# Order of the first two token groups in the K/V stage of a pre-norm transformer layer

## The reference

```
k = layernorm(x) @ wk + bk      # [4096, 2048] x [2048, 512]
v = layernorm(x) @ wv + bv      # the same shape
```

## Time and profile before

| | us |
|---|---|
| median of 3 runs | 2394.8 (2394.18 to 2396.35) |
| the profiled execution's own time | 2397.82 |
| its span (slowest core, core 6) | 2396.3 |
| the other cores' spans | 2388.2 to 2394.7 |
| K of group 2 begins on core 6 | 119.11 after the span's start |
| group 2 of stage A, with `own_ln` beside it | 32.17 (119.11 to 151.28) |
| group 3, without it | 32.17 (151.28 to 183.45) |
| one step of `own_ln` on VectorE | 1.22 |

### The profile page before, as it was taken

How to read it: one execution, slowest core, us unless ns; L and a number is a source line. 1 busy time by engine, 2 the same in 40 slices (tenths; PEclk the granted TensorE clock), 3 DMA queues, 4 the chain that set the end, 5 groups by cost and what they waited for, 6 DMA issues and landing times.

```text
span 2396.3 us, 32016 instructions; the slowest of 8 cores (2388.2 to 2396.3 us)
## 1 busy us (share of the span) xinstructions
PE 2319.0 (97%) x11140; PEld 1016.3 (42%) x11364; DVE 824.9 (34%) x1505; ACT 621.6 (26%) x789; POOL 78.6 (3%) x148
## 2 busy tenths in 40 slices
PE   5899999999999999999999999999999999999999
PEld 2344433333333443444444444444444444444444
DVE  2432245566554335323333332111333333333101
ACT  1444437777776332111111110000111111110000
POOL 2000000000000000000000000000000000000000
PEclk9999999999999999999999999999999999999999
DMA  9624111111355830522443237776223442234872
GB/s 160 104 36 71 18 27 19 19 19 27 66 84 107 193 112 1 100 52 51 84 84 61 45 57 140 163 165 148 50 53 65 84 79 47 48 74 85 184 158 89
DMA packets 57285, 193.46 MB, mean 81 GB/s; under 512 B 10246, under 2 KB 14854, under 8 KB 48940
## 3 DMA queue, kind: packets, MB, share of 16 engines
q0 software_dynamic: 23808, 139.99, 34.1%
q1 hardware_dynamic: 33324, 51.40, 6.7%
HBM read 306.18 MB, written 25.18 MB: 138 GB/s over the span
## 4 chain that ended last, share of the span: by engine, by line
PE 90%; DMA 3%; issue 2%; ACT 2%; DVE 1%; another core or an unknown queue 1%; POOL 0%; DVEq 0%; ACTq 0%; SPq 0%; POOLq 0%
PE pq L1275 32%; PE pq L1437 15%; PE pq L900 5%; PE pq L729 5%; PE pq L453 4%; PE pq L414 4%; PE pq L628 4%; PE pq L1302 4%; PE pq L1287 4%; PE pq L1353 4%; PE pq L781 4%; DMA wkv_wv<-wv_h 2%; PE pq L799 2%; DMA out_d<-dx_stg 1%; ACT wc_p L742 1%
## 5 line engine op out<-in xcount | busy, mean ns | idle before, releaser
L1275 PE MATMUL pq<-dv_xln,dw_wsl 128*128 128x512 bf16 x3513 | 804.7, 379 | 4.3 <-ACT ds_s L1320 0.3
L1275 PEld LDWEIGHTS pq<-dv_xln,dw_wsl 128*128 128x128 bf16 x3584 | 350.2, 98 | 424.5 <-issue 3.7
L1437 PE MATMUL pq<-dx_x2s,dw_wsl 128*128 128x512 bf16 x1754 | 388.4, 379 | 5.6 <-DVE dx_stg L1455 2.2
L1320 ACT ACTIVATE ds_s<-pq 128x512 bf16<-128x512 f32 x112 | 66.9, 597 | 939.1 <-PE pq L1302 884.3
L1337 DVE TENSOR_TENSOR ds_x<-ds_s,pq 128x512 bf16<-128x512 bf16 x108 | 74.3, 688 | 650.6 <-PE pq L1302 614.8
L742 ACT ACTIVATE wc_p<-pq,gl_nb 128x1024 bf16<-128x1024 f32 (+4 forms) x252 | 256.2, 1046 | 71.9 <-PE pq L729 65.6
L1437 PEld LDWEIGHTS pq<-dx_x2s,dw_wsl 128*128 128x128 bf16 x1792 | 174.7, 98 | 216.8 <-issue 7.2
L1455 DVE TENSOR_TENSOR dx_stg<-pq,dx_stg 128x512 f32<-128x512 f32 x64 | 42.0, 688 | 334.6 <-PE pq L1437 141.9
L781 PE MATMUL pq<-wc_p,pp_V 128*128 128x512 bf16 (+3 forms) x493 | 139.6, 363 | 1.1 <-DVE pl_p L753 0.2
L1287 PE MATMUL pq<-dp_c,dw_wsl 128*128 128x512 bf16 x438 | 131.1, 379 | 2.2 <-DVE dp_d L1098 1.7
L1302 PE MATMUL pq<-dp_d,dw_wsl 128*128 128x512 bf16 x440 | 131.3, 379 | 1.6 <-DVE xg_x L1328 1.0
(11 more groups left out here) (183 smaller groups left out, 1750.6 us busy)
## 6 DMA issues: line engine op xcount, KB each, us to landing
dw_wsl<-w_h POOLq DMA_DIRECT2D x56, 1216.0 KB, 10.0
dw_wsl<-w2b_h POOLq DMA_DIRECT2D x16, 960.0 KB, 10.8
dw_wsl<-w2a_h POOLq DMA_DIRECT2D x16, 896.0 KB, 9.6
wa_xr<-x_tiles POOLq DMA_DIRECT2D x6, 2048.0 KB, 40.2
wc_wq<-wq_h POOLq DMA_DIRECT2D x16, 512.0 KB, 5.7
dw_ev<-xo_oc SPq DMA_DIRECT2D x32, 256.0 KB, 6.1
wo_w<-wo_h POOLq DMA_DIRECT2D x16, 512.0 KB, 14.8
xres_d<-dw_ev SPq DMA_DIRECT2D x32, 256.0 KB, 6.1
```

The lines of the kernel that those rows point to most:

```text
L1275: ms = [(lambda hc, bank=bank, wo_=wo_: (lambda e: e.matmul(bank[:, 0:TD], w[:, wo_ + hc * 128: wo_ + (hc + 1) * 128], xln2[tt][:, hc * TD ...
L1437: ms.append((lambda j=j, t=t: (lambda e: e.matmul(banks[t][:, 0:TD], w[:, j * 128:(j + 1) * 128], x2s[:, j * 2 * TD + t * TD: j * 2 * TD + ...
```

## The change

It moves work of groups 0 and 1 and changes banks; the arithmetic of every product stays the same.

- **Loads:** x of group 1 is asked for ahead of W_v.
- **Group 1's K directly behind group 0's.** Its four heads use `pb[4]`, `pb[5]`, `pb[0]`, `pb[1]`. Heads 0 and 1 are computed in pieces, between the steps of group 0's `moments`, `turn_row`, `k_out` and `k_norm`; heads 2 and 3 whole.
- **W_v's column sums** come behind `moments(1)`, in `pb[2]`; their copy goes to a buffer of its own, `csv`, that lies over V rows of group 6.
- **V of both groups behind that**, in `pb[2]` and `pb[3]`. The four centrings of W_v on VectorE alternate with `k_out(1, p)`. From group 2 on K is in `pb[0]` to `pb[3]` and V in `pb[4]`, `pb[5]`, as before.
- **`own_ln`** of groups 0 and 1 runs during groups 2 and 3 instead of 1 and 2.
- `moments` now calls `put` once, between its copy (L360) and its two matmuls.

```diff
-        c_k, c_v = pb[0:4], pb[4:6]
+        def k_bank(j, kv):
+            return (pb[4], pb[5], pb[0], pb[1])[kv] if j == 1 else pb[kv]
+        def v_bank(j, sub):
+            return pb[(2 if j < 2 else 4) + sub % 2]
...
-        def moments(j, put=(lambda i: None)):
+        def moments(j, put=(lambda: None)):
...
             v = P.g('vector', [lambda e: e.tensor_copy(stA, st_b[:, 0:CK])], waits=[('pe', s1_pe[j])], inc='ve')
+            put()
...
-            put(0)
...
-            put(1)
...
         wk_tok = load_w(wk_sb, wk_h, 'K')
         load_x(0)
+        load_x(1)
         wv_tok = load_w(wv_sb, wv_h, 'V')
-        for j in range(1, 5):
+        for j in range(2, 5):
             load_x(j)
...
-        tot = col_sums(wv_sb, wv_tok, c_v[1])
-        wvs = P.g('scalar', [lambda e: e.activation(out=rs_t[1], in_=c_v[1][:, 0:512], func=AF.Copy)],
-                  waits=[tot], inc='sc')
-        moments(0, lambda i: centre(wv_sb, i, rs_t[1], ('sc', wvs), 'v'))
-        for sub in range(2):
-            v_mm(0, sub, 0, 4)
+        kp1 = {}
+        def k_piece(p):
+            for kv in range(2):
+                kp1[kv] = k_mm(1, kv, 4 * p, 4 * p + 4)
+        squares(1, 0)
+        moments(0, lambda: k_piece(0))
+        squares(1, 1)
+        sums(1, 0)
+        k_piece(1)
         trn = turn_row(0)
-        squares(1, 0)
-        for p in range(1, 4):
...
-        squares(1, 1)
-        v_out(0, 2, v_mm(0, 2))
+        turned(0, trn)
+        k_out(0, 0, kp0[0])
+        k_out(0, 1, kp0[1])
         sums(1, 1)
+        squares(1, 2)
+        k_piece(2)
+        k_out(0, 2, kp0[2])
+        k_out(0, 3, kp0[3])
         k_norm(0)
-        squares(1, 2)
-        v_out(0, 3, v_mm(0, 3))
         sums(1, 2)
         squares(1, 3)
-        for j in range(1, NCK):
+        k_piece(3)
+        kp1[2] = k_mm(1, 2)
+        sums(1, 3)
+        def third_k():
+            kp1[3] = k_mm(1, 3)
+        moments(1, third_k)
+        for p in range(4):
+            tot = col_sums(wv_sb, wv_tok, pb[2], p, [('sc', kb_sc[(0, 2)])] if p == 0 else [])
+        csv_sc = P.g('scalar', [lambda e: e.activation(out=csv, in_=pb[2][:, 0:512], func=AF.Copy)],
+                     waits=[('pe', tot)], inc='sc')
+        trn = turn_row(1)
+        turned(1, trn)
+        for p in range(4):
+            centre(wv_sb, p, csv, ('sc', csv_sc), 'v')
+            k_out(1, p, kp1[p])
+            vpe = [v_mm(0, sub, 4 * p, 4 * p + 4) for sub in range(2)]
+        k_norm(1)
+        v_out(0, 0, vpe[0])
+        v_out(0, 1, vpe[1])
+        for sub in range(2, 4):
+            v_out(0, sub, v_mm(0, sub))
+        squares(2, 0)
+        for sub in range(4):
+            v_out(1, sub, v_mm(1, sub))
+            sums(2, sub)
+            if sub < 3:
+                squares(2, sub + 1)
+        for j in range(2, NCK):
...
-                if j == 1 and kv == 2:
-                    turned(1, turn_row(1))
-                if j <= 2:
-                    own_ln(j - 1, kv)
+                if j <= 3:
+                    own_ln(j - 2, kv)
```

More of the change, by code:

```diff
@@ L179, in build_program @@
         bvr_sb = WA.al('bvr', [128, 512], F32)
+        csv = Arena(nc, SB0 + 58 * KBB, SB0 + 60 * KBB, 'vs').al('csv', [128, 512], F32)
         rbA = [V_sb[:, 28 * 512 + j * 1024:28 * 512 + (j + 1) * 1024] for j in range(2)]
@@ L313, in load_w, with col_sums @@
                                          src[:, p * 2048:(p + 1) * 2048], sem=f'd{tag}{p}')) for p in range(4)]
[L315 to L321, removed]
+        def col_sums(w, toks, bank, p, free=()):
+            return P.g('tensor', [(lambda hc: (lambda e: e.matmul(
+                bank[:, 0:512], onb_sb, w[:, hc * 512:(hc + 1) * 512],
+                start=(hc == 0), stop=(hc == NCH - 1), skip_group_check=True)))(hc)
+                for hc in range(4 * p, 4 * p + 4)], waits=[toks[p], ('dC1', d_c1), *free], inc='pe')
         def centre(w, p, total, tok, key):
@@ L407, in k_mm @@
             wts = []
-            if kv == 0 and j == 0:
+            if j == 0 and kv == 0:
                 wts += [x_tok[0][lo // 4], ('ve', ctr_ve[('k', lo // 4)])]
-            elif kv == 0:
+            elif j == 1:
+                wts.append(x_tok[1][(hi - 1) // 4])
+            elif j >= 2 and kv == 0:
                 wts += x_tok[j]
-            if j and lo == 0:
+            if lo == 0 and j == 1:
+                wts.append(('ve', ctr_ve[('k', 3)]) if kv < 2 else ('sc', kb_sc[(0, kv - 2)]))
+            elif lo == 0 and j == 2:
+                wts.append(('sc', kb_sc[(1, kv + 2)]) if kv < 2 else ('ve', vev_ve[(1, kv)]))
+            elif lo == 0 and j:
                 wts.append(('sc', kb_sc[(j - 1, kv)]))
             return P.g('tensor', [(lambda hc: (lambda e: e.matmul(
-                c_k[kv][:, 0:CK], wk_sb[:, hc * 512 + kv * 128: hc * 512 + (kv + 1) * 128],
+                k_bank(j, kv)[:, 0:CK], wk_sb[:, hc * 512 + kv * 128: hc * 512 + (kv + 1) * 128],
                 x_view(j)[:, hc, :], start=(hc == 0), stop=(hc == NCH - 1), skip_group_check=True)))(hc)
@@ L421, in k_out @@
             kv_ve[(j, kv)] = P.g('vector', [
-                lambda e: e.tensor_mul(c_k[kv][:, 0:CK], c_k[kv][:, 0:CK], rs_t[j % 2]),
+                lambda e: e.tensor_mul(k_bank(j, kv)[:, 0:CK], k_bank(j, kv)[:, 0:CK], rs_t[j % 2]),
             ], waits=[('pe', pe), ('sc', rs_sc[j])], inc='ve')
@@ L425, in k_out @@
             kb_sc[(j, kv)] = P.g('scalar', [
-                lambda e: e.activation(out=ks, in_=c_k[kv][:, 0:CK], func=AF.Identity, bias=bk_sb[:, kv:kv + 1]),
+                lambda e: e.activation(out=ks, in_=k_bank(j, kv)[:, 0:CK], func=AF.Identity, bias=bk_sb[:, kv:kv + 1]),
             ], waits=[('ve', kv_ve[(j, kv)]), ('dCon', d_consts)], inc='sc')
@@ L449, in v_mm @@
             if n == 0:
-                wts.append(('ve', ctr_ve[('v', lo // 4)]))
-            elif n >= 2:
+                wts += [('ve', ctr_ve[('v', lo // 4)]), ('sc', csv_sc)]
+            elif n == 1:
+                wts.append(('sc', kb_sc[(0, 3)]))
+            elif 8 <= n < 10:
+                wts.append(('sc', kb_sc[(1, n - 8)]))
+            else:
                 wts.append(('ve', vev_ve[((n - 2) // 4, (n - 2) % 4)]))
             v_pe[j] = P.g('tensor', [(lambda hc: (lambda e: e.matmul(
-                c_v[sub % 2][:, 0:512], x_view(j)[:, hc, sub * 128:(sub + 1) * 128],
+                v_bank(j, sub)[:, 0:512], x_view(j)[:, hc, sub * 128:(sub + 1) * 128],
                 wv_sb[:, hc * 512:(hc + 1) * 512],
@@ L462, in v_out @@
             vev_ve[(j, sub)] = P.g('vector', [lambda e: e.scalar_tensor_tensor(
-                V_sb[:, ci * 512:(ci + 1) * 512], c_v[sub % 2][:, 0:512], rtok[j % 2][:, sub:sub + 1], bvr_sb,
+                V_sb[:, ci * 512:(ci + 1) * 512], v_bank(j, sub)[:, 0:512], rtok[j % 2][:, sub:sub + 1], bvr_sb,
                 op0=ALU.mult, op1=ALU.add)],
@@ L478, in build_program @@
         load_x(0)
+        load_x(1)
         wv_tok = load_w(wv_sb, wv_h, 'V')
-        for j in range(1, 5):
+        for j in range(2, 5):
             load_x(j)
         z_ve = P.g('vector', [lambda e: e.memset(nsw, 0.0)], inc='ve')
-        tot = col_sums(wk_sb, wk_tok, c_v[0])
         for p in range(4):
-            centre(wk_sb, p, c_v[0][:, 0:512], tot, 'k')
+            tot = col_sums(wk_sb, wk_tok, pb[4], p)
+        for p in range(4):
+            centre(wk_sb, p, pb[4][:, 0:512], ('pe', tot), 'k')
@@ L486, in build_program @@
         for p in range(4):
             squares(0, p)
-            kpe = [k_mm(0, kv, 4 * p, 4 * p + 4) for kv in range(NKV)]
+            kp0 = [k_mm(0, kv, 4 * p, 4 * p + 4) for kv in range(NKV)]
             sums(0, p)
-        tot = col_sums(wv_sb, wv_tok, c_v[1])
-        wvs = P.g('scalar', [lambda e: e.activation(out=rs_t[1], in_=c_v[1][:, 0:512], func=AF.Copy)],
-                  waits=[tot], inc='sc')
-        moments(0, lambda i: centre(wv_sb, i, rs_t[1], ('sc', wvs), 'v'))
-        for sub in range(2):
-            v_mm(0, sub, 0, 4)
@@ L498, in build_program @@
-        trn = turn_row(0)
-        squares(1, 0)
-        for p in range(1, 4):
[L501 to L510, removed]
-        squares(1, 1)
-        v_out(0, 2, v_mm(0, 2))
+        kp1 = {}
@@ L524, in build_program @@
                 if kv == 0:
-                    if j == 1:
-                        sums(1, 3)
                     moments(j)
```

## The result

The changed kernel's median is 2424.09 us (16 runs), that of the kernel before beside it 2395.61 (16 runs). Every comparison here leaves out the runs in which a whole die was slower (5 of the changed kernel's 16), and the ratio of the rest is 1.0062, interval 1.0040 to 1.0085. That ratio holds two things: of the 11 runs seven lie at 2400.7 to 2403.1, median 2402.2, and four at 2424 to 2426, in which one or two pairs of neighbouring cores (2 and 3, 6 and 7) were 20 us and more longer at a granted clock of 0.983. Two further series of the same kernel had no such run in 17 and gave 1.0024 (1.0014 to 1.0033) and 1.0022 (1.0011 to 1.0032): **slower by 5 to 6 us, clear of noise and just over 0.2%**.

The account below looks back on a forecast made before the run. TensorE, busy 97% of the span, was taken as the bound. Group 2 at 116.8 at full clock plus 3.6 for clock falls gives 120.4, against the mean core's 117.65 +2.75: 2394.8 + 2.8 = 2397.6 us, range 2392.5 to 2402.

Parts of the forecast that it names:

- Loads* (1): Load queue: x of group 1 takes W_v's early places, W_v lands by about 64 us, and no load is waited for.
- Dense part* (4): TensorE from k_norm(0) to W_v's column sums: 15.3 us without a wait, ending at 77.1; 4.5 us of W_v waits gained.
- Gaps* (2, 3, 5, 6): TensorE idles 2.95 us before sums(1, 0), 6.0 before k_norm(0), 3.0 around turn_row(1), 3.2 between V pieces, 1.8 around k_norm(1).
- the stretch at full clock, with its waits: From the end of K of group 0, 43.8, to the start of group 2, 116.8, without any clock fall.
- fall at the first gap: Lower clock behind the 2.95 us wait ahead of sums(1, 0): half of 1.6, 0.8 us.
- fall at the second gap: Lower clock behind the 6.0 us wait ahead of k_norm(0), with dense work following: 2.6 us.
- fall at the third gap: Lower clock behind the wait around turn_row(1), mostly hidden by VectorE's pace of 2.8: 0.2 us, at most 0.9.
- The term for the clock: Slower matmuls behind the three gaps, in sum 3.6 us, moving the start of group 2 from 116.8 to 120.4.
- the first rival: Every gap fells the clock at full price, 6.1 us: group 2 at 122.9, kernel 2400.1; chance 0.29.
- no fall: Rival: no clock fall on the path, group 2 at 116.8, kernel 2393.9; chance 0.18.
- no queueing at k_norm: Rival: ScalarE gets the k_out pairs in ahead, so the 6.0 us gap and its 2.6 go: 2389.0; chance 0.05.
- x lands late: Rival: x of group 1 arrives late and TensorE waits behind K of group 0, up to 8 us: 2403; chance 0.03.

Follow-up runs that it names:

- a0: The changed kernel again beside the kernel before: stretch (end of K of group 0 to start of group 2) 78.6 us, ratio 1.0024.
- a7: The changed kernel once more, unaltered, beside the kernel before, to look for the cluster at 2424: stretch 78.5 us, ratio 1.0022.
- a5: The changed kernel with only the loads in their old order, W_v ahead of x of group 1: ratio 1.0074, group 2 starts at 135.2.
- b1: The changed kernel with all three gaps filled together by reordering K pieces, k_norm, column sums, centrings and V pieces: 2386.04 us, ratio 0.9958, stretch 64.1.
- b4: The changed kernel with only k_norm(1) moved behind V's third and fourth block: stretch 76.8 us, ratio 1.0011.
- a4: The changed kernel with 24 matmuls that nothing reads added in the gap ahead of k_norm(0): stretch 76.6 us, ratio 1.0016.
- a1: The changed kernel with k_norm(0) moved behind the fourth K piece and head two of group 1: stretch 76.1 us, ratio 1.0007.
- b2: b1 with k_norm(0) and the sums put back ahead of the K piece and head two: stretch 71.4 us, ratio 0.9993.
- a3: The changed kernel with the second K piece of group 1 put ahead of sums(1, 0): stretch 76.6 us, ratio 1.0013.
- a2: The changed kernel with W_v's column sums and three of four centrings moved ahead of head two of group 1: stretch 79.0 us, ratio 1.0020.

## Why the prediction was wrong

**The steps that held, in kind.** *Loads* (1): no wait for W_v, and x of group 1 in time. *Dense part* (4): no wait. *Gaps* (2, 3, 5, 6): all of them stand where the walk had them, on the engines that it named, and the V pieces are 2.8 apart. own_ln and everything from group 2 on: no change, as forecast (core 0 of the changed kernel takes 32.16 and 32.17 us for groups 2 and 3).

**What failed is two sizes in the sum.** The table sets what the sum took beside what the stretch holds, as the mean of the eight cores, in the first profile and in those of a0 and a7.

| us | taken | first | a0, a7 |
|---|---|---|---|
| the stretch at full clock, with its waits | 73.0 | 74.7 | 74.7, 74.7 |
| fall at the first gap | 0.8 | 2.1 | 1.6, 1.4 |
| fall at the second gap | 2.6 | 1.7 | 1.4, 1.6 |
| fall at the third gap | 0.2 | 0 | 0, 0 |
| fall on V's 48 matmuls behind k_norm(1) | none | 1.1 | 0.8, 0.8 |
| sum | 76.6 | 79.6 | 78.6, 78.5 |

- **The term for the clock, 3.6 us at three places, was 4.9, 3.9 and 3.8.** Two of its parts were too small. For the first gap I took half of 1.6 because core 0 of the kernel before kept its clock through a like wait; in the changed kernel all eight cores fell, all eight again in a0 and six in a7. The trace of before had the odds: behind the wait ahead of turn_row the 24 V matmuls took 6.9 to 7.0 us on six cores and 5.41 on cores 0 and 4 alone, and core 0's wait there was 2.42 us against core 6's 2.96. The fall on V's last 48 matmuls of group 0 was put at nothing without a reason: it came on 5, 4 and 4 of the eight cores (12.21 for 10.52). The second gap was taken too high by about 1, and that this nearly balances the other two in a0 and a7 is luck.
- **The waits were taken 1.7 us too short.** Each of these is the same on every core of all three profiles: 6.69 us from the end of K of group 0 to sums(1, 0) for 6.35; 8.77 from turn_row's end to k_norm(0) for 8.3; 8.14 from W_v's sums to the first V piece for 7.46; 12.63 from there to V's third block for 12.4. Each is a chain over two or three engines, and each was walked a few tenths too fast.
- **A slip of bookkeeping, 0.45**: I walked from core 6's 43.8 and compared with the mean of the eight cores, whose K of group 0 ends at 44.25.

Forecast for the mean core were 2.75 us; the stretch grew by 6.2 in the first profile and by 5.1 to 5.2 in the other two. The three items make up that difference.

So the first rival (every gap fells the clock, group 2 at 122.9, 2400.1, chance 0.29) comes nearest: 123.3 to 124.2. Its mechanism is what happened on most cores: the first fall reached turn_row on three cores of the first profile, and on all eight the slower matmuls ahead of turn_row moved the ScalarE chain back. That its time fits is luck in part: its 6.1 us for the clock are 1.2 to 2.3 too high, and the waits and the slip, which it shares with my forecast, are 2.2 too low. The Trainium skill's rule (TensorE: Matmul & The Clock Gate, HAM oscillation — how this bites in real kernels), that bursts behind waits start cold, agrees with 22 of the 24 core traces of the changed kernel at the first gap. The rivals "no fall", "no queueing at k_norm" and "x lands late" are out; a5 shows what the last would have looked like.

**Open** is the cluster at 2424. It makes up some 22 of the 26.5 us between my forecast and the first series' median, no profile shows it, and what caused it is not known.

**What the change was worth, then.** Its idea works once the order is put right: b1 keeps its loads, its banks and K of group 1 first, and beats both kernels. No run closes the gaps of the kernel before with its loads as they were, so how much of b1's 10 us the loads bring, and how much the order alone would, is open. What lost in the change was the order on TensorE's queue: matmuls that were ready stood behind k_norm(0), turn_row(1) and k_norm(1), which wait for the two slower engines.

## What to carry to other kernels

When work is moved up to cover a transfer, look where the small steps stand that wait for another engine: everything ready behind them on the same queue is stopped too, so put the large ready blocks ahead of them. Price such a wait with the slower matmuls behind it, and read from all cores how often the clock fell, not from the one that got away. Close gaps that lie close together in one edit before you judge any of them: one closed alone gave 0 to 2.5 us here, one left open cost 7.3. And look into the timelines before you read a small difference of two profiles as an effect: b4's was worth 2.4 us and more where the totals showed 1.8.

## What the runs showed of the hardware

- Added work can shorten a stretch: 5.3 us of unused matmuls in a wait of 6.3 us let the 24 matmuls behind it run in 5.35 us for 6.16 to 6.97, worth 1.5 to 1.8 us at that place by the granted clock alone (a4).
- The gains did not add: 2.5, 0 and 2.0 us for single edits, 1.8 for k_norm(1), 14.5 for b1 (78.6 to 64.1), which moves a little more than the four. The cleaner pair is one edit in two kernels: k_norm(0) moved gave 2.5 us with the other gaps open (a1) and 7.3 with them closed (b1 against b2).
- A fall can move to the next wait rather than go away: with the second gap closed, 16 matmuls behind a wait of 2.62 us took 4.8 to 5.3 us on every core (a1); with the first gap cut to 1.35 us, the next K piece fell on five of eight cores (a3).
- A wait as short as 1.61 us cost V's 48 matmuls 1.7 us on 13 of 24 core traces behind thinly spread V pieces (the changed kernel), and on none of eight behind a dense block of 32 (a2).
